# The second router's logits as eight more columns of two products, and the projection tile by tile

## The reference, cut to what matters

```python
x = x + 0.5 * ffn(layernorm(x))          # first router, first expert stage
x = x + attn(layernorm(x))
x = x + 0.5 * ffn(layernorm(x))          # second router, second expert stage

# ffn: xf = 8192 rows
scores = softmax(xf @ router_w)          # router_w: 256 x 8
weights, experts = top_k(scores, 2)      # each expert takes its first 1024 rows, per choice
out += weight * (gelu(row @ w1[e]) @ w2[e])

# attn
q, k, v = split(x @ w_qkv.T)             # rotary scaling of q, k; 16 heads of 16
y = ((q k^T / 4) * decay_mask) v         # then normalised over each head's channels and all tokens
out = (silu(x @ w_gated.T) * yn) @ w_proj.T
```

## Time and profile before

| what | us |
|---|---|
| median of 3 runs | 2314.96 (2314.14 to 2319.64) |
| the profiled execution | 2312.59 |
| its span, first to last instruction | 2310.8 |
| busy: PE, PEld, DVE, ACT, POOL | 2170.1, 1907.2, 1358.5, 1003.8, 1171.7 |
| mean granted clock of PE | 0.977 |

### The profile page before, as it was taken

One profiled execution on the slowest core, in us unless ns is written; L12 is line 12 of the kernel. 1 busy time (PEld: TensorE's weight loads), 2 busy tenths in 40 slices (PEclk: granted clock), 3 DMA queues, 4 the chain that ended last, 5 costly groups with the idle time before them and its releaser, 6 DMA issues.

```text
span 2310.8 us, 57931 instructions
## 1 busy us (share of the span) xinstructions
PE 2170.1 (94%) x22549; PEld 1907.2 (83%) x22549; DVE 1358.5 (59%) x3312; ACT 1003.8 (43%) x2149; POOL 1171.7 (51%) x911
## 2 busy tenths in 40 slices
PE   7869999999999997999999999849999999999998
PEld 6759999999999987777777777638999999999997
DVE  7755555555555552578778877645555555555553
ACT  4434434343434342446555555434344444444442
POOL 5755777735354533223344453454777654444443
PEclk9999999999999998999999999869999999999999
DMA  9523444434343424102211121123444443434432
GB/s 365 211 81 68 101 93 99 99 87 98 82 104 81 105 55 119 39 21 76 76 40 59 59 77 75 60 81 94 100 92 102 90 101 86 100 87 99 89 80 32
DMA packets 138440, 211.52 MB, mean 92 GB/s; under 512 B 34092, under 2 KB 114544, under 8 KB 132080
## 3 DMA queue, kind: packets, MB, share of 16 engines
q0 software_dynamic: 57344, 69.21, 17.9%
q1 hardware_dynamic: 80912, 139.72, 17.5%
HBM read 138.13 MB, written 72.88 MB: 91 GB/s over the span
## 4 chain that ended last, share of the span: by engine, by line
PE 52%; DVE 4%; issue 2%; ACT 1%; another core or an unknown queue 0%; POOL 0%; DMA 0%; POOLq 0%; DVEq 0%; ACTq 0%
PE bank L675 16%; PE bank L657 15%; PE bank L768 10%; PE bank L856 3%; PE bank L889 1%; PE bank L824 1%; PE bank L644 1%; PE bank L839 1%; PE bank L874 1%; PE bank L928 1%; PE bank L786 1%; DVE aw L1829 0%; DVE rt L1817 0%; DVE xnl L1803 0%
## 5 line engine op out<-in xcount | busy, mean ns | idle before, releaser
L1167 ACT ACTIVATE h<-bank 128x512 f32<-128x512 f32 x512 | 306.1, 598 | 850.9 <-PE bank L657 740.0
L1738 DVE CAST hh<-h 128x512 fp32r<-128x512 f32 x512 | 241.2, 471 | 692.6 <-ACT h L1167 578.8
L675 PE MATMUL bank<-w2h,hh 128*128 128x256 f32 x2048 | 579.1, 283 | 3.1 <-ACT yb L1185 3.1
L675 PE MATMUL bank<-w2h,hl 128*128 128x256 f32 x2048 | 573.7, 280 | 0.0
L675 PE MATMUL bank<-w2l,hh 128*128 128x256 f32 x2048 | 573.7, 280 | 0.0
L675 PEld LDWEIGHTS bank<-w2h,hh 128*128 128x128 f32 x2048 | 385.1, 188 | 45.4 <-ACT yb L1185 3.6
L675 PEld LDWEIGHTS bank<-w2h,hl 128*128 128x128 f32 x2048 | 384.8, 188 | 41.5
L675 PEld LDWEIGHTS bank<-w2l,hh 128*128 128x128 f32 x2048 | 385.2, 188 | 39.4
L657 PE MATMUL bank<-xh,w1h 128*128 128x512 f32 x1024 | 405.1, 396 | 2.0 <-issue 1.7
L657 PE MATMUL bank<-xh,w1l 128*128 128x512 f32 x1024 | 404.3, 395 | 0.0
L657 PE MATMUL bank<-xl,w1h 128*128 128x512 f32 x1024 | 404.1, 395 | 0.0
(11 more groups left out here) (215 smaller groups left out, 3305.0 us busy)
## 6 DMA issues: line engine op xcount, KB each, us to landing
stg<-in_L_ffn_w SPq DMA_DIRECT2D x64, 1024.0 KB
xb<-acc SPq DMA_DIRECT2D x9, 1024.0 KB
xa<-in_L_attn_x SPq DMA_DIRECT2D x8, 1024.0 KB, 14.4
xn_rows<-xa SPq DMA_DIRECT2D x8, 1024.0 KB
xn_rows<-xn_r SPq DMA_DIRECT2D x8, 1024.0 KB
xr<-acc SPq DMA_DIRECT2D x7, 1024.0 KB
out_rows<-xr SPq DMA_DIRECT2D x7, 1024.0 KB
slot_table<-pay,idx POOLq DMA_INDIRECT x256
```

The costliest lines, as they stand in the source:

```text
L675: product = pe.matmul(tile_sum(j, t, end), a[:, fj, t * P:(t + 1) * P], c[:, fj, :], start=(fj == 0 and i == 0 and (end or t % 2 == 0)), s ...
L1167: act.activation(h32[fj % 2][:], bank[fj % 2][:], ACT.Gelu_apprx_tanh).then_inc(f.gelu, 1)
L1738: dve.tensor_copy(hh[:, fj, :], h32[fj % 2][:]).then_inc(f.hh, 1)
```

## The change

The layer norm before the router is a shift and a scale of each row, so the logits are the scale times the row times a router matrix whose columns have mean zero (`rwc`). The row is the input row of the attention block plus the projection's output. Its first part's logits come as eight columns behind the value product, its second part's as eight columns behind the projection, whose eight weight columns are `w_proj` times `rwc`.

- Before `ffn(0)`: PE and DVE make `rwc` and the mixed columns (six small matmuls, five DVE operations), split in high and low parts.
- `project_values` has 264 columns; ACT copies the eight new ones to `part`, scaled by `spread` (the standard deviation, one more DVE operation per batch in `front_shift`). SP stores `part` to DRAM and loads it into columns 256 to 263 of `xr` (`part_store`, `part_load`), because the tokens lie in another order there. `residual(b, 0)` waits for that load too.
- `out_pair` becomes `out_tile`: eight per batch of 264 columns, each with its own bank use, its own `residual` and `residual_stats`.
- `residual_pair`, `residual_evac`, `logits`, its copy, `logits_back` and `rwide` are gone. `residual_choices` reads the logits from `xr`, without the scale, which does not change their order; `exponent_scale` (two DVE operations) puts it in for the exponents.
- DVE's order: `residual_choices(b-2)` moves to the start of the sequence, `exponent_scale` stands where it was; each `residual(b-1, j)` stands by itself, four of them ahead of `mask`, `rotate`, `slot_entries` and `carry` steps; `residual_variance(b-1)` and `residual_shift(b-1)` come later, behind `carry(n+8, 0)` and `channel_stats(n+6)`.
- In the drain DVE routes a first, before the statistics of z; z's choices come before its last four statistics; POOL's `residual_power(z)` stands behind the scatters of a.
- `xr` and `xb` have 264 columns in a row, so the 1 MB transfers move pieces of 1 KB in SBUF.

```diff
@@ -50,11 +50,11 @@
 
 def bank_of(kind, b, j):
 
-    if kind == "gate" or kind in ("out", "residual") and b == B - 1:
+    if kind == "gate" or kind == "out" and b == B - 1:
         return 1 + j % 2
-    if kind in ("logits", "back", "counts") and b >= B - 2:
+    if kind == "counts" and b >= B - 2:
         return 0
-    return 2 if kind in ("turn", "front", "residual") else 1
+    return 2 if kind in ("turn", "front") or kind == "out" and j == 1 else 1
...
-        rw, rwide = sb("rw", [P, KC, E]), sb("rwide", [P, KC, 32])
-
-        wTh, wTl = sb("wTh", [P, KC, 5 * C], f32r), sb("wTl", [P, KC, 5 * C], f32r)
-        W_QK, W_V, W_G, W_P = 0, 2 * C, 3 * C, 4 * C
+        rw, rwc = sb("rw", [P, KC, E]), sb("rwc", [P, KC, E])
+
+        wTh, wTl = sb("wTh", [P, KC, 5 * C + 2 * E], f32r), sb("wTl", [P, KC, 5 * C + 2 * E], f32r)
+        W_QK, W_V, W_G, W_P = 0, 2 * C, 3 * C + E, 4 * C + E
+        W_VR, W_PR = W_V + C, W_P + C
...
+            def part_store(b):
+
+                sp.wait_ge(A.v_r, nth[1]["values", b, NT - 1])
+                sp.dma_start(part_t[b, :, :, :], part[:, b % 2]).then_inc(A.part, 16)
+
+            def part_load(b):
+
+                sp.wait_ge(A.part, b * 16 + 16)
+                if b >= 1:
+                    sp.wait_ge(R[1].link, (b - 1) * LINKS + EXP_LINK)
+                sp.dma_start(rows_of(b)[:, :, C:C + E], part_w[b, :, :, :]).then_inc(R[1].x_last if b == B - 1 else R[1].x, 16)
...
                     residual_load(b - 1)
+                    part_store(b - 1)
+                    part_load(b - 1)
...
+            for k in range(KC):
+                last = pe.matmul(bank[4][:, 0:E], ones[:], rw[:, k, :], start=(k == 0), stop=(k == KC - 1))
+            last.then_inc(S0.wT, 1)
+            pe.wait_ge(S0.bias, 2)
+            for k in range(KC):
+                for j in range(KC):
+                    last = pe.matmul(bank[5][:, k * E:(k + 1) * E], wraw[:, 8 + j, k * P:(k + 1) * P], rwc[:, j, :],
+                                     start=(j == 0), stop=(j == KC - 1))
+            last.then_inc(S0.wT, 1)
+            pe.wait_ge(S0.wTl, 22)
...
-                split_product(o[:, 0:C], *x_parts(i * P, P), *w_parts(W_V, C)).then_inc(full, 1)
+                split_product(o[:, 0:C + E], *x_parts(i * P, P), *w_parts(W_V, C + E)).then_inc(full, 1)
...
+            def out_tile(b, j):
+
+                if not 0 <= b < B:
+                    return
+                pe.wait_ge(A.ygl, b * KC + (j // 2 + 1 if b == B - 1 else KC))
                 o, full = claim("out", b, j)
-                for t in range(2):
-                    s = slice((2 * j + t) * P, (2 * j + t + 1) * P)
-                    last = split_product(o[:, t * C:(t + 1) * C], lambda k: ygh[:, k, s], lambda k: ygl[:, k, s], *w_parts(W_P, C))
-                last.then_inc(full, 1)
-
-            def residual_pair(b, j):
-
-                if not 0 <= b < B:
-                    return
-                pe.wait_ge(R[1].xn, b * NT + 2 * j + 2)
-                o, full = claim("residual", b, j)
-                for t in range(2):
-                    for k in range(KC):
-                        last = pe.transpose(o[:, (t * KC + k) * P:(t * KC + k + 1) * P], xn_r[:, 2 * j + t, k * P:(k + 1) * P], ident)
-                last.then_inc(full, 1)
-
-            def logits(b):
-
-                if not 0 <= b < B:
-                    return
-                for j in (NT // 2 - 2, NT // 2 - 1):
-                    m = bank_of("residual", b, j)
-                    pe.wait_ge(frees[m], nth[m]["residual", b, j])
-                if b == 0:
-                    pe.wait_ge(S0.base, 6)
-                o, full = claim("logits", b, 0)
-                for k in range(KC):
-                    for g in range(4):
-                        last = pe.matmul(o[g * 32:(g + 1) * 32, 0:2 * P], rwide[:, k, :], xrT[:, 2 * g:2 * g + 2, k, :],
-                                         start=(k == 0), stop=(k == KC - 1), skip_group_check=True)
-                last.then_inc(full, 1)
-
-            def last_logits():
-
-                z = B - 1
-                o, full = claim("logits", z, 0)
-                for gs in (range(3), range(3, 4)):
-                    for g in gs:
-                        m = bank_of("residual", z, g)
-                        pe.wait_ge(frees[m], nth[m]["residual", z, g])
-                    for k in range(KC):
-                        for g in gs:
-                            last = pe.matmul(o[g * 32:(g + 1) * 32, 0:2 * P], rwide[:, k, :], xrT[:, 2 * g:2 * g + 2, k, :],
-                                             start=(k == 0), stop=(k == KC - 1), skip_group_check=True)
-                last.then_inc(full, 1)
-
-            def logits_back(b):
-
-                if not 0 <= b < B:
-                    return
-                o, full = claim("back", b, 0)
-                for j in range(2):
-                    last = pe.transpose(o[:, j * P:(j + 1) * P], lg[:, j * P:(j + 1) * P], ident)
-                last.then_inc(full, 1)
+                s = slice(j * P, (j + 1) * P)
+                split_product(o[:, 0:C + E], lambda k: ygh[:, k, s], lambda k: ygl[:, k, s], *w_parts(W_P, C + E)).then_inc(full, 1)
...
+                b, i = n // NT, n % NT
+                if i == 0:
+                    act.wait_ge(A.lnnm, b + 1)
+                    if b >= 2:
+                        act.wait_ge(A.part, (b - 1) * 16)
+                act.activation(dst, o[:, 0:C].rearrange("p (m a y) -> p m a y", a=2, y=D), ACT.Copy)
+                act.activation(part[:, b % 2, i, :], o[:, C:C + E], ACT.Copy, scale=spread[:, b % 2, i:i + 1]).then_inc(free, 1)
...
+            def exponent_scale(b):
+
+                if not 0 <= b < B:
+                    return
+                S = R[1]
+                dve.wait_ge(S.lnrs, b + 1)
+                dve.wait_ge(S.link, b * LINKS + EXP_LINK)
+                dve.tensor_tensor(dls[:], dl[:], over_e(lnr.rs[:]), ALU.mult).then_inc(S.scaled, 1)
+                dve.wait_ge(S.scaled, 2 * b + 1)
+                dve.tensor_scalar(dls[:], dls[:], -87.0, None, ALU.max).then_inc(S.scaled, 1)
...
+                dve.tensor_tensor(spread[:, b % 2, :], lnf.rv[:], lnf.rs[:], ALU.mult)
+                norm_shift(A, lnf, b)
...
-                two = rows_of(b)[:, 2 * j:2 * j + 2, :].rearrange("p t c -> p (t c)")
-                dve.tensor_tensor(two, two, bank[m][:], ALU.add).then_inc(frees[m], 1)
+                dve.tensor_tensor(rows_of(b)[:, j, :], rows_of(b)[:, j, :], bank[m][:, 0:C + E], ALU.add).then_inc(frees[m], 1)
...
             def drain():
 
                 a, z = B - 2, B - 1
+                residual_choices(a)
+                choice_part(a, 0)
+                exponent_scale(a)
+                choice_part(a, 1)
+                places(a, 0)
                 channel_stats(B * NT - 1)
                 channels(z)
                 about_head(z)
+                places(a, 1)
+                places(a, 2)
                 head_variance(z)
+                places(a, 3)
+                places(a, 4)
                 affine(z)
+                slot_entries(1, a)
                 last_gating(0)
                 last_gating(1)
                 last_low(0)
                 last_gating(2)
                 last_low(1)
                 residual(z, 0)
-                residual_stats(z, 0)
+                residual(z, 1)
                 last_gating(3)
                 last_low(2)
-                residual(z, 1)
+                residual(z, 2)
+                residual(z, 3)
+                last_low(3)
+                residual_stats(z, 0)
                 residual_stats(z, 1)
-                last_low(3)
-                residual(z, 2)
+                residual(z, 4)
+                residual(z, 5)
                 residual_stats(z, 2)
-                residual(z, 3)
                 residual_stats(z, 3)
-                residual_variance(z)
-                residual_choices(a)
-                choice_part(a, 0)
-                residual_shift(z)
-                choice_part(a, 1)
-                for part in range(5):
-                    places(a, part)
-                slot_entries(1, a)
+                residual(z, 6)
+                residual(z, 7)
                 residual_choices(z)
                 choice_part(z, 0)
                 choice_part(z, 1)
-                for part in range(5):
+                places(z, 0)
+                for j in range(4, NT):
+                    residual_stats(z, j)
+                residual_variance(z)
+                places(z, 1)
+                residual_shift(z)
+                exponent_scale(z)
+                for part in range(2, 5):
                     places(z, part)
                 slot_entries(1, z)
```

More of the change, by code:

```diff
@@ L367, in _ @@
             residual_load(B - 1)
+            part_store(B - 1)
+            part_load(B - 1)
             residual_store(B - 2)
@@ L1429, in drain @@
                 last_high(0)
-                logits_copy(a)
```

(6 more changed lines are left out.)

199 lines of the change are left out of this document (87 added, 112 removed).

## The result

The changed kernel takes 2338.4 us (median of 7 runs, 2335.4 to 2344.4), the kernel before 2316.8 in the same session (7 runs): ratio 1.009, 95% interval [1.007, 1.011]. The forecast was 2304, faster; the time lies above its range. The profiled execution of the changed kernel took 2339.0 us (span 2337.2) against 2312.6.

The account below looks back on a forecast made before the run. PE was 94% busy but DVE paced first halves and small-step chains the end. Batches -5.6, drain -5.9, setup +0.3 gave -11 us: 2312.6 to 2301.4, plus 2.4 for the median, 2304; range 2283 to 2322 (8 in 10).

Parts of the forecast that it names:

- What bounds the kernel: Whole kernel: PE busy 94%, but DVE paces the first half of a batch and small-step chains set the end.
- Removed and added on PE: PE per batch: some 3.7 us of rows removed, 0.36 us of wider products and 0.4 us of matmul-kind changes added.
- First half: First half of a batch: PE's savings end in its wait for a mask; gain nothing, between 0 and 1 us.
- power, scatters and additions late: Rival: POOL's late power and scatters delay its additions, which hold DVE, 2.5 us in seven batches; 2326 us, chance 0.13.
- Second half: Second half of a batch: new waits, then PE catches up; gain 0.8 us per batch, 5.6 us over seven.
- `spread` and `exponent_scale`: New DVE operations that POOL additions could hold: 0.16 us at least, 1.1 at most each; 0.2 taken.
- The drain: After the last batch: statistics of z come 5.4 us late, yet `idx` of z 5.9 us earlier; gain 5.9 us.
- Setup: Before the expert stages: new weight preparation mostly hidden in PE's wait for rows; cost 0.3 us.
- The transfers: Rival: small transfers behind the 1 MB load come late, DVE stands still 3 us in seven batches; 2325 us, chance 0.04.
- signs of error: Repeat under 70 us, PE waiting for POOL at `turn(n+1)`, DVE for a DMA at first residual, longer way to last residual.

Follow-up runs that it names:

- e11: Changed kernel with POOL's half-bias additions moved later, choice steps moved into the second half, a new drain order and the small transfers issued first: ratio 0.9989 to before.
- e12: e11 with DVE making channel means and second mask ahead of the first choice steps, and PE making head variances behind the projection: 2301.5 us, ratio 0.9946.
- second pair: Both kernels unaltered, measured and profiled again on chips where the kernel before takes 2293 us: changed 2320.9 us, ratio 1.012; before 2293.1 us.
- e1: Changed kernel with the two first choice steps put back directly ahead of the exponent's scaling on DVE: ratio 1.012 to before.
- e6: Changed kernel with idle transposes on PE ahead of its waits at head means, head variances and counts: ratio 1.0115 to before.
- e3: Kernel before with a dummy 1.8 us DVE reduction behind the first mask of batches 2 to 7: ratio 1.0033, +7.6 us.
- e5: Changed kernel with POOL's first two half-bias additions of each batch moved behind the power of the head variances: 2306.5 us, ratio 1.0051 to before.
- e9: e5 with choice steps, scan, counts and places moved from the first half of a batch into the second: ratio 1.0139 to before.
- e4: Changed kernel with POOL's first two half-bias additions moved behind the power of the head variances for batch a in the drain only: ratio 1.0125 to before.

## Why the prediction was wrong, step by step

**What bounds the kernel: right.** DVE paced the first half; e11 and e12 gain by taking work and order out of there.

**Removed and added on PE: right in sign, too high.** Forecast 3.7 us out and 0.8 in, 2.9 a batch. At clock 1.00 on both sides it is 1.9 (397.3 to 385.9). The removed rows add up to 21.8 us in six batches, as forecast, but the products of 264 columns take 3.8 us more than those of 256, where I had 2.2, and nearly every other kind of row has grown a little. Rows overlap their neighbours, so these sums do not add up to the 11.4.

**First half: the step that failed.** I wrote that `residual_choices` moves ahead of `channels`, two steps of 0.25 us, that the head statistics come 0.5 us late, and "Gain of the first half: nothing, between 0 and 1". Measured: the subtraction alone made them 1.8 us late, PE waited 1.3 us at `head_means`, and the batch came out 3.2 us longer (4.8 in the second pair) instead of 0.8 shorter.

Three errors lie in it. First, I priced two steps by their length where nothing disturbs them; the additions of POOL had moved onto them. I had that as a rival (power, scatters and additions late, 2326 us, chance 0.13), with the mechanism and place right and a price of 1.1 us twice instead of one hold of 2 us; the moved additions gave 14.4 us back, of the 26.8 that the changed kernel loses on that chip. Of the Trainium skill's rule (SBUF — State Buffer, section "SBUF: two separate sides") I had looked at the two new operations only; the hold in e1 fell on a one-input step that was there before, so I would now ask it of every step under a POOL addition. The same sentence of that section also names DVE operations in a two-port mode, which I had left out; whether the step in e1 ran in such a mode, no run here shows.

Second, I took a longer wait of PE as free. In six batches the changed kernel spends 20.8 us more of busy time than e12 on the same work, at clock 0.94 instead of 1.00; how much of that reaches the time, e6 could not settle.

Third, the turned rows that were removed had been what PE did while DVE was late: with them a delay of 1.9 us costs 0.9 to 1.3 (e3), without them the hold costs 2.0 a batch (e5). This reading is argued from the two runs; none puts the rows back.

These three do not make up the whole loss. The 12 us that e5 leaves, with the late norms on ACT among the candidates, stay unpriced piece by piece.

**Second half: not tested by itself.** Forecast 0.8 us gained per batch. It can't be read apart from the late first half; e12's six batches are 1.8 us each shorter than before on a chip of nearly the same speed (417.8 against 428.6), but it also carries other edits.

**`spread` and `exponent_scale`: right in the batches, wrong in the drain.** 0.16 and 0.2 us in the batches; 3.05 for the scaling of a.

**The drain: right but for one hold.** Forecast: the statistics of z 5.4 us late, and `idx` of z 5.9 earlier all the same. Counted from DVE's last mask, the statistics come 8.8 us late in the first pair of profiles (3.2 to 11.9) and 8.0 in the second (3.2 to 11.2); 2.8 of that is the hold on the scaling of a. `idx` of z comes 2.6 us earlier in the first pair (47.2 to 44.6) and 3.4 in the second (47.3 to 43.9): about the forecast gain less that hold. From the head means of z to its `idx` the gain is 10.8 (42.5 to 31.7 us) in either pair, where I had 11.3.

**Setup.** Forecast 0.3. The first product of the first expert stage came 1.9 us later in the first pair of profiles (and the first head means 2.6), 0.2 in the second; kernels with the same setup gave 151.0 to 155.1 on the chip of 2320 us. Open, and small.

**The transfers.** Forecast as a rival with 0.04: in the changed kernel one wait of 1.24 us. But they had no room: as soon as DVE was 4 to 6 us earlier at the first residual, counted from the head means (e9), it waited 2.9 to 4.2 us for them in each batch.

Of the signs of error that I had named, only the wait of DVE for a DMA at the first residual came (1.24 us, once). PE waits for POOL at `turn` once, 1.06 us at the very first tile (928.67), where the kernel before waits 1.71 (926.99); in the second profile five more such waits of 0.23 to 0.28 us appear. All are small; the wait that mattered stood at `head_means`, which I had not named. What makes up the rest between the moved additions (1.0051) and the kernel before is settled by e11 and e12 as a whole (late choices, order of the first half, transfers), not piece by piece.

## What to carry to other kernels

When work is removed from the busiest engine, ask at each place whether that engine or another sets the pace there: where another did, the removed work was filler, and here its absence went with longer waits and a lower granted clock for the work behind them (0.94 instead of 0.98). When a result comes later than before (here the variance, with the eighth tile), follow every queue that waits for it to the large GpSimd operation at its end, and look at what VectorE does under it then. Do the same for ScalarE's queue. A fix that frees one engine wants the small transfers checked next: their order in the queue was right only as long as the engine was late.

## What the runs showed of the hardware

A VectorE operation on two columns with a single SBUF input and an SBUF output took 1.98 us under two GpSimd additions in a row instead of 0.17 (e1), and a 64-column one 3.05 instead of 0.20. That one began while a GpSimd scatter ran, 0.5 us ahead of the additions, and ended with them; beside a scatter alone (e4, 1501.28) it took 0.20. The hold lasts to the end of the run of additions, 2.5 us for two, not of the first; in e11, under three such additions in a row (1201.94 to 1205.69), statistics (0.74 us) and an operation that reads PSUM (0.69) kept their length. PE's granted clock went to 0.50 in the changed kernel behind three waits of 0.95, 1.30 and 1.22 us (1208 to 1215) and in e11 behind two of 0.85 and 1.22; in e12, with 21 waits of 0.8 us in the mean over six batches, its mean was 1.00; idle transposes put into the waits shortened the slow stretch but did not remove it.
